# First experts with three mask banks and three buffers of chosen rows, last experts over 71 tiles

## The reference

```python
x = x + _L0_xattn_ref(_layernorm(x), ctx_1024, ctx_1024, ...)     # softmax attention over the context
x = x + _L0_ffn_ref(_layernorm(x), L0_ffn_gate_w, L0_ffn_expert_w)
x = x + _L1_xattn_ref(_layernorm(x), ctx_1024, ctx_1024, ...)     # the same with a causal mask
x = x + _L1_ffn_ref(_layernorm(x), router_w, gate_proj, up_proj, down_proj)

# _L0_ffn_ref: each row goes through the one expert with the highest score (a 128x128 matrix)
scores = jnp.einsum('bsh,eh->bse', x, gate_w)
onehot = jax.nn.one_hot(jnp.argmax(scores, axis=-1), 8)
expert_out = jnp.einsum('bsh,efh->bsef', x, expert_w)
return x + jnp.einsum('bsef,bse->bsf', expert_out, onehot)

# _L1_ffn_ref: each row goes through its best two of 8 experts, F = 352, weighed by their softmax shares
routing_weights, routing_idx = jax.lax.top_k(softmax(x @ router_w), 2)
acts = silu(gate) * up            # 128 -> 352 each
expert_out = acts @ down_proj     # 352 -> 128
```

## Time and profile before

| what | value |
|---|---|
| median of 3 runs (lowest, highest) | 699.16 us (696.54, 702.19) |
| profiled execution, its own time | 697.68 us |
| its span | 695.9 us |
| mean granted TensorE clock | 0.950 |
| busy share of TensorE, VectorE, ScalarE, GpSimd | 86%, 68%, 55%, 49% |

### The profile page before, as it was taken

One profiled execution on the slowest core, in us unless ns is written; L12 is line 12 of the kernel. 1 busy time (PEld: TensorE's weight loads), 2 busy tenths in 40 slices (PEclk: granted clock), 3 DMA queues, 4 the chain that ended last, 5 costly groups with the idle time before them and its releaser, 6 DMA issues.

```text
span 695.9 us, 22954 instructions
## 1 busy us (share of the span) xinstructions
PE 597.2 (86%) x8205; PEld 458.9 (66%) x8205; DVE 476.5 (68%) x1287; ACT 380.1 (55%) x900; POOL 338.0 (49%) x593
## 2 busy tenths in 40 slices
PE   1888399999998999997999988898779999999960
PEld 1555277777664555454667766676569899999960
DVE  2777578888835766677778889888656855555536
ACT  3788167777771344442577676677444344444420
POOL 3666332222412454352333677667638886555540
PEclk9999689999999999998899999999769999999995
DMA  7468827565781055767344423400112232222119
GB/s 192 134 189 193 208 69 158 156 162 147 216 168 59 19 231 159 272 210 279 143 93 113 104 80 93 103 26 29 48 47 77 64 82 71 64 69 67 51 43 351
DMA packets 65407, 87.66 MB, mean 126 GB/s; under 512 B 11528, under 2 KB 52752, under 8 KB 65296
## 3 DMA queue, kind: packets, MB, share of 16 engines
q1 hardware_dynamic: 55736, 74.84, 38.8%
q0 software_dynamic: 4352, 8.99, 4.0%
q10 hardware_dynamic: 5208, 2.36, 1.2%
HBM read 43.99 MB, written 41.96 MB: 124 GB/s over the span
## 4 chain that ended last, share of the span: by engine, by line
PE 56%; DVE 20%; issue 6%; ACT 3%; DMA 2%; SPq 0%; DVEq 0%; ACTq 0%; POOL 0%; POOLq 0%
PE bank L1810 12%; PE bank L814 7%; PE bank L1818 6%; DVE nm L1059 6%; PE bank L1664 5%; PE bank L769 4%; PE bank L795 3%; PE bank L798 3%; PE bank L752 2%; PE bank L835 2%; PE bank L825 2%; PE bank L831 2%; DMA kk<-results 1%; DVE e0ch L1633 1%; PE bank L1459 1%
## 5 line engine op out<-in xcount | busy, mean ns | idle before, releaser
L929 ACT ACTIVATE pr<-bank 128x512 f32<-128x512 f32 x256 | 154.3, 605 | 81.5 <-PE bank L798 78.7
L1059 DVE TENSOR_REDUCE nm<-bank 128x8 f32<-128x1024 f32 x128 | 155.6, 1221 | 33.2 <-PE bank L769 30.3
L1810 PE MATMUL bank<-exxt,qq 128*128 128x128 f32 (+1 forms) x864 | 110.0, 278 | 1.1 <-ACT exxt L1851 0.7
L1810 PEld LDWEIGHTS bank<-exxt,qq 128*128 128x128 f32 (+1 forms) x864 | 101.6, 185 | 2.3 <-ACT exxt L1851 1.1
L1783 POOL DMA_INDIRECT results<-exy,exre x72 | 72.0, 1000 | 25.4 <-issue 25.4
L814 PE MATMUL bank<-pr,wide_values 128*18 128x128 f32 x2048 | 83.0, 281 | 0.0
L1664 PE MATMUL bank<-e0ch,expert_w 128*128 128x512 f32 x128 | 70.5, 633 | 7.4 <-DVE e0ch L1633 7.4
L795 PE MATMUL bank<-qq,kk 48*128 48x128 bf16 x1024 | 75.9, 222 | 0.4 <-ACT pr L929 0.4
L798 PE MATMUL bank<-mt,pick 64*128 64x128 bf16 x1024 | 76.0, 222 | 0.0
L1889 DVE TENSOR_TENSOR exhi<-bank,exsi 128x384 f32<-128x384 f32 x72 | 40.1, 557 | 49.2 <-PE bank L1810 40.3
L1340 POOL DMA_INDIRECT sorted_in<-rrrow,rrpli x64 | 62.9, 983 | 16.5 <-issue 15.3
(11 more groups left out here) (246 smaller groups left out, 1101.1 us busy)
## 6 DMA issues: line engine op xcount, KB each, us to landing
sorted_in<-values SPq DMA_DIRECT2D x25, 715.0 KB, 5.9
kk<-k_parts SPq DMA_DIRECT2D x64, 96.0 KB
qq<-q_parts SPq DMA_DIRECT2D x64, 96.0 KB
exx<-sorted_in SPq DMA_DIRECT2D x72, 65.0 KB
kk<-k_parts SPq DMA_DIRECT2D x64, 64.0 KB
qq<-q_parts SPq DMA_DIRECT2D x64, 64.0 KB
k_parts<-pj_parts SPq DMA_DIRECT2D x8, 384.0 KB, 3.4
q_parts<-pj_parts SPq DMA_DIRECT2D x8, 384.0 KB, 3.7
```

The source lines that it names most:

```text
L929: act.activation(probs[c], st_bank[(n * NC + c) % ST][:], ACT.Exp, scale=scale).then_inc(exp_s, 1)
L1059: dve.tensor_reduce(neg_max[n % 2][:, u * 2 * C4:(u + 1) * 2 * C4], score_banks(n, u).rearrange("q (h k) -> q h k", k=T), AX_X, ALU.max, n ...
L1810: mm = pe.matmul(to[q.p][0:fn, f * T:(f + 1) * T], own_w[q.p][:, w0 + f0:w0 + f0 + fn], x, start=True, stop=True)
```

## The change

Two edits that do not touch each other.

1. **First experts.** The masks get three banks (2, 3 and now 6) and the chosen rows three buffers. TensorE issues spread 2 of a group behind turn_back, ahead of expert 0, and behind expert e it issues spread e+3 where it issued e+2. The waits on banks and buffers reach three back instead of two. Bank 6 held the turned queries of groups 0 to 6; these now go to bank 0, the bank of the turned rows, so turn_queries waits until the turned rows of the group after have been kept, and turn waits until the queries turned before have been kept. The wait for the cross attention's last use of bank 6 moves from turn_queries to spread 2 of the first group.
2. **Last experts.** The loops over tiles end after 71 (64 whole tiles plus at most 7 begun ones). The lists still have 72 slots, the last group still fetches and turns four tiles.

```diff
@@ -40,6 +40,8 @@
 F = 352
 FCH = ((0, 128), (128, 128), (256, 96))
 SLOTS = 2 * B + E
+
+TILES = 2 * B + E - 1
 ROW = D + 2
 LIST = B * T + T
 SPARE = 2 * B * T
@@ -140,6 +142,7 @@
 SURE = 5
 EARLY = (2 * SURE * BMAX - (E - 1)) // G * G
 LATE = SLOTS - EARLY
+SPREAD = 3
 LAST_BATCH, BEFORE_LAST = BATCHES[-1], BATCHES[-2]
 LATE_TURN, LATE_SCORE, LATE_SHARE, LATE_COUNT, LATE_LIST = 3, 5, 8, 9, 11
 
@@ -152,6 +155,7 @@
                 return batch, j // 2, j % 2
     return None
 LAST_TILES = Group(NQ // 2 - 1, 1)
+LAST_TILE = Seq(LAST_TILES, (TILES - 1) % G)
 
 
 class Stage:
@@ -1422,10 +1426,10 @@
             top, best = two("top", [128, G]), two("best", [128, G])
             tie, ranked = two("tie", [128, G, E]), two("rk", [128, G, E])
             hot = two("hot", [128, G, E], BF16)
-            chosen = two("ch", [128, GT])
+            chosen = [sb(f"e0ch{p}", [128, GT], to=own) for p in range(SPREAD)]
             padding = values[0][:].rearrange("p b d -> p (b d)")[:, 0:PAD * ROW].rearrange("p (n d) -> p n d", d=ROW)
             t_bank, sc_bank, hot_bank, y_bank, z_bank, qt_bank, q_bank = (
-                bank[0], bank[1], bank[2:4], bank[4], lambda g: bank[7 if g.n < LAST.n else 4], lambda g: bank[6 if g.n < LAST.n else 4], lambda g: bank[5 if g.n < LAST.n else 4])
+                bank[0], bank[1], (bank[2], bank[3], bank[6]), bank[4], lambda g: bank[7 if g.n < LAST.n else 4], lambda g: bank[0 if g.n < LAST.n else 4], lambda g: bank[5 if g.n < LAST.n else 4])
 
             def x_of(g):
                 return x_res[:, g.n * G:(g.n + 1) * G, :]
@@ -1443,10 +1447,10 @@
                 mm.then_inc(z_ps, 1)
 
             def turn_queries(pe, g):
-                if g.n == 0:
-                    pe.wait_ge(cross.norm_s, B)
                 pe.wait_ge(q_ln.xn_s, g.n + 1)
                 pe.wait_ge(q_kept, earlier(g.n))
+                if g.n < LAST.n:
+                    pe.wait_ge(kept, min(g.n + 3, NG))
                 for t in range(G):
                     mm = pe.transpose(qt_bank(g)[:, t * T:(t + 1) * T], q_ln.xn[g.p][:, t, :], ident[:])
                 mm.then_inc(q_turned, 1)
@@ -1509,6 +1513,7 @@
                     pe.wait_ge(cross.max_s, B * (NC // 2))
                 pe.wait_ge(ln.xn_s, g.n + 1)
                 pe.wait_ge(kept, earlier(g.n))
+                pe.wait_ge(q_kept, earlier(g.n - 2))
                 for t in range(G):
                     mm = pe.transpose(t_bank[:, t * T:(t + 1) * T], ln.xn[g.p][:, t, :], ident[:])
                 mm.then_inc(turned, 1)
@@ -1527,9 +1532,11 @@
                     pe.wait_ge(cross.exp_s, B * NC)
                 if e == 0:
                     pe.wait_ge(hot_s, g.n + 1)
-                pe.wait_ge(chosen_s, earlier(g.n * E + e - 1))
+                if g.n == 0 and e == 2:
+                    pe.wait_ge(cross.norm_s, B)
+                pe.wait_ge(chosen_s, earlier(g.n * E + e - SPREAD + 1))
                 for t in range(G):
-                    mm = pe.matmul(hot_bank[e % 2][:, t * T:(t + 1) * T],
+                    mm = pe.matmul(hot_bank[(g.n * E + e) % SPREAD][:, t * T:(t + 1) * T],
                                    hot[g.p][:, t, e:e + 1].broadcast_to([128, 128]), ident4[:, 0, :],
                                    start=True, stop=True)
                 mm.then_inc(hot_ps, 1)
@@ -1629,8 +1636,9 @@
                 def choose(g, e):
 
                     dve.wait_ge(hot_ps, g.n * E + e + 1)
-                    dve.wait_ge(y_ps, earlier(g.n * E + e - 1))
-                    dve.tensor_tensor(chosen[e % 2][:], hot_bank[e % 2][:], xn_t[g.p][:], ALU.mult).then_inc(chosen_s, 1)
+                    k = (g.n * E + e) % SPREAD
+                    dve.wait_ge(y_ps, earlier(g.n * E + e - SPREAD + 1))
+                    dve.tensor_tensor(chosen[k][:], hot_bank[k][:], xn_t[g.p][:], ALU.mult).then_inc(chosen_s, 1)
 
                 def body(g, first=False, last=False):
                     choose(g, 0)
@@ -1661,16 +1669,17 @@
                     pe.wait_ge(chosen_s, g.n * E + e + 1)
                     if e == 0:
                         pe.wait_ge(y_s, earlier(g.n))
-                    pe.matmul(y_bank[:], expert0_w[:, e, :], chosen[e % 2][:], start=(e == 0), stop=(e == E - 1)
+                    pe.matmul(y_bank[:], expert0_w[:, e, :], chosen[(g.n * E + e) % SPREAD][:], start=(e == 0), stop=(e == E - 1)
                               ).then_inc(y_ps, 1)
 
                 def body(g, first=False, last=False):
                     if not first:
                         turn_back(pe, g.before())
+                    spread(pe, g, SPREAD - 1)
                     for e in range(E):
                         expert(g, e)
-                        if e + 2 < E:
-                            spread(pe, g, e + 2)
+                        if e + SPREAD < E:
+                            spread(pe, g, e + SPREAD)
                         if e == 3 and not last:
                             turn(pe, g.after())
                         if e == 5 and not last:
@@ -1785,7 +1794,7 @@
                         y_g[q.b][:], None).then_inc(y_out[q.b], 16)
 
                 def body(g):
-                    for t in range(G):
+                    for t in range(min(G, TILES - g.n * G)):
                         routed.late_gpsimd(g.n * G + t)
                         send(Seq(g, t))
                 all_groups(pool, body, NQ)
@@ -1842,7 +1851,7 @@
                 body(FIRST, first=True)
                 middle_groups(pe, body, NQ)
                 body(LAST_TILES, last=True)
-                down(Seq(LAST_TILES, G - 1), expert_of(pe, Seq(LAST_TILES, G - 1)))
+                down(LAST_TILE, expert_of(pe, LAST_TILE))
 
             def on_scalar(act):
                 def keep_turned(g):
@@ -1879,7 +1888,7 @@
                 body(FIRST, first=True)
                 middle_groups(act, body, NQ)
                 body(LAST_TILES, last=True)
-                keep_out(Seq(LAST_TILES, G - 1))
+                keep_out(LAST_TILE)
 
             def on_vector(dve):
                 def activate(q):
@@ -1909,9 +1918,9 @@
                     dve.tensor_tensor(result[g.p][:].unsqueeze(2), tags, aside[:].unsqueeze(2), ALU.add).then_inc(tags_s, 1)
 
                 def body(g, last=False):
-                    for t in range(G):
+                    for t in range(min(G, TILES - g.n * G)):
                         activate(Seq(g, t))
-                        if not (last and t >= G - 2):
+                        if g.n * G + t + 2 < TILES:
                             take_weights(Seq(g, t).ahead(2))
                         routed.late_vector(g.n * G + t)
                         if t == G - 1 and not last:
@@ -1929,7 +1938,7 @@
                 body(LAST_TILES, last=True)
 
             stage = Stage(on_sync, on_tensor, on_scalar, on_vector, on_gpsimd)
-            stage.results_out = [(y_out[t], 16 * NQ) for t in range(G)]
+            stage.results_out = [(y_out[t], 16 * len(range(t, TILES, G))) for t in range(G)]
             return stage
 
         def combine(x_dst, ran):
```

## The result

| kernel | median, us | runs (lowest, highest) | profiled execution, its span | clock |
|---|---|---|---|---|
| before | 699.01 | 6 (696.54, 702.19) | 697.68, 695.9 | 0.950 |
| changed | 693.94 | 6 (692.71, 696.12) | 692.71, 690.9 | 0.951 |

The ratio is 0.994, with a 95% interval of 0.9912 to 0.9968. The change makes the kernel faster by 0.3 to 0.9%, less than the 1% that one measurement can tell from no change. The two profiled executions differ by 5.0 us, the medians by 5.1.

The account below looks back on a forecast made before the run. A loop of VectorE and TensorE, closed through ScalarE, was taken to bound the first experts, TensorE the last. Savings of 2.1 us there and 2.0 for the tile gave 699.16 - 4.1 = 695.1 us, range 691.0 to 699.0.

Parts of the forecast that it names:

- The loop that bounds the stage: First experts: VectorE from query_rest to choose 3, TensorE to queries, then ScalarE; one spread less saves 0.22 us a group.
- Zero for the buffers: First experts: the extra bank and buffer gain nothing; choose 5's 0.84 us wait goes, but nobody waits for it.
- The cover before expert 1: First experts: TensorE's 0.59 us wait before expert 1 absorbs the added spread, which delays expert 0 by some 0.05 us.
- The new waits: First experts: turn_queries' wait for keep_turned has 2.1 us of room, turn's wait is for queries long kept; no cost.
- The room at turn: First experts: narrowest place, ScalarE's apply ends at 274.32 and turn starts at 274.45, leaving 0.13 us.
- First group: First experts' opening group: the added spread fits in 0.98 us of idle time before expert 0, so 0.22 us is gained.
- Last group: First experts' final group, without stats: choose 3 and expert 3 come 0.32 us earlier, plus 0.22 us behind expert 3: 0.54 us.
- The tile: Last experts: one tile less saves 2.00 us of TensorE, from below 1.33 us.
- Only the tile counts: First experts: another wait, most likely turn, closes the 0.22 us, leaving 697.2 us; chance 0.12.
- The bubbles are a lack of buffers: First experts: waits before experts 1 and 3 both go, 7.7 us in all, giving 687.4 us; chance 0.07.
- Less low clock: Start of causal attention: the half-clock stretch at 325 to 335 us goes, worth 2.4 us, giving 692.7; chance 0.12.

Follow-up runs that it names:

- The fifth run: Choose 3 put ahead of query_stats in VectorE's list, against the changed kernel: one execution 692.16 us, period 13.74 us.
- e0y: Not a follow-up run: a buffer in the profile rows, read by TensorE's transposes at L1446 and waited for from ScalarE; no measured time of its own.
- the tile alone: The kernel before with 71 tiles in the last experts and nothing else changed: median 696.32 us against 699.77, ratio 0.9967.
- the third run: The changed kernel with three mask banks and three buffers, but each spread at its old place: one execution 695.07 us, period 14.05 us.
- spaced chooses: The changed kernel with GpSimd's bias moved behind row_rstd and VectorE's chooses 1, 2 and 3 each moved earlier: median 688.35 us against 699.39, ratio 0.9846.
- the first experts' part alone: The changed kernel with 72 tiles in the last experts: median 695.6 us against 699.77 of before, ratio 0.9927.
- bias later: The changed kernel with GpSimd's bias of the group before moved behind the next row_rstd: one execution 691.85 us, period 13.77 us.

## Why the prediction was right

The forecast was 695.1 us in a range of 691.0 to 699.0, and 693.94 was measured. In the two traces the stage's 2.37 us are 0.11 up to the first turn_back (0.22 foreseen), 1.69 over the six middle periods (1.32 foreseen) and 0.57 in the last group (0.54 foreseen). Both traces have low clock in the first group and not of the same shape, so the 0.11 can't be split. Point by point:

- **The loop that bounds the stage.** Right. The distance of VectorE's part is unchanged (5.42 us), TensorE's from expert 3 to queries is 0.27 us shorter. One spread accounts for 0.22. The rest is score: behind a spread it was 0.86 us from its start to that of turn_queries, in TensorE's timeline before (277.98 in the earlier trace rows):

```profile
277.12 1.01 PE L1520 MATMUL bank<-gate_w,e0xt 128*128 128x8 f32 x8
```

  Behind an expert it is 0.81 (276.16 to 276.97 above). The others of groups 2 to 6 have 0.86 or 0.87 and 0.81 or 0.82. I had counted the spread and not what the step behind it gains; why score is shorter there is not shown.
- **Zero for the buffers.** Right for the middle groups, shown from both sides: depth without the new place gives a period of 14.05, the new place without the third buffer 13.77. In the last group the third buffer gives 0.23 us. I had put that group's whole 0.54 us on the place of the spread, and a part of it belongs to the buffer, through choose 2.
- **The cover before expert 1.** Right. The wait is still there, and in four of the five groups 2 to 6 it is 0.54 or 0.55 us from the end of the spread's 0.22 us to the expert, where I had expected about 0.5:

```profile
282.57 0.39 PE L1539 MATMUL bank<-ident,e0hot 128*128 128x128 bf16 x4
283.34 1.12 PE L1672 MATMUL bank<-e0ch,expert_w 128*128 128x512 f32 x2 [0.38 <-DVE e0ch L1641]
```

  In the period shown further up it is 0.35. There turn_back is late: one step of route (L1567, at 263.83) took 0.64 us where it takes 0.34 to 0.36 in those others, and choose 7, expert 7 and turn_back came later for it, but query_rest did not. So choose 1 starts 1.48 us behind turn_back (267.38 to 268.86), and started 1.68 us behind it before (267.91 to 269.59). The period did not change, which shows that the cover was enough. A spread behind turn_back starts 0.49 us after it, where I had reckoned with 0.44.
- **The new waits.** Right: neither turn nor turn_queries waits for the other's bank.
- **The room at turn.** 0.13 us was read off rows as if a start could follow an end at once. The fifth run shows that about half of such a distance is the handover. It did not matter at this change, since apply and expert 3 both follow from query_rest: apply starts 5.57 us behind it now (266.40 to 271.97) and started 5.54 behind it before (267.13 to 272.67). It decides the next one.
- **First group.** The added spread fitted into the idle time ahead of expert 0, which is now 0.76 us:

```profile
212.39 1.26 PE L1672 MATMUL bank<-e0ch,expert_w 128*128 128x512 f32 x2 [0.76 <-DVE e0ch L1641]
...
214.16 2.08 PE L1672 MATMUL bank<-e0ch,expert_w 128*128 128x512 f32 x2
```

- **Last group.** Expert 3 comes 4.19 us behind its turn_back and not 4.53. Queries come 0.58 us sooner behind those before them, for 0.54 foreseen:

```profile
308.48 0.65 PE L1446 MATMUL bank<-ident,e0y 128*128 128x128 f32 x4 [0.23 <-ACT e0y L1703]
...
312.67 1.12 PE L1672 MATMUL bank<-e0ch,expert_w 128*128 128x512 f32 x2
```

- **The tile.** 2.00 us foreseen; 2.16 between the first gate_up and the last send, and 2.2 for the tile alone.
- **The rivals.** "Only the tile counts" is refuted by the stage's own 2.37 us and by the period. "The bubbles are a lack of buffers" is refuted by the changed kernel together with the third run, and with it, for this stage, the reading that I had taken from the Trainium skill, "Perfetto Trace Analysis", Optimization Strategy: the gap repeated before expert 3 in every group, and a third bank and buffer left it at 0.42 us. What took it away were two moves in the lists of VectorE and GpSimd. "Less low clock" came in part: the low stretch at the start of the causal attention took 10.2 us of the trace before and 6.8 of the one after, and the stretch up to the first causal output projection was 0.32 us shorter. That it came of the change is not shown. Windows after, which answer to the earlier trace rows:

```profile
325.00:330.00 5.00, 3.02 (x47) 2.22 (x43) 3.56 (x6) 1.13 (x4) 0.00 (x0) 0.59 1.02 416
330.00:335.00 5.00, 5.00 (x93) 3.40 (x87) 2.89 (x3) 1.83 (x5) 1.34 (x2) 0.73 0.88 353
```

Between the 4.1 us foreseen and the 5.0 of the two traces stand 0.3 us of the stage, 0.2 of the tile, 0.3 of the clock and 0.3 behind the last send, less 0.2 lost before the stage; that is 0.9.

## What to carry to other kernels

A wait that comes back in every turn of a loop is read from the engine that feeds it: if that engine has no idle time ahead of its instruction, as here, more banks and buffers don't take the wait away, and the order of its list is the next thing to try. When two ways close a loop within a tenth of a microsecond of each other, neither edit shows anything alone, so try them together before either is dropped; and a distance between a recorded end and a start that depends on it is room only beyond the handover that a waiting pair of the same kind shows. What a spread, a tile or a wait is worth below 1% is read from landmarks between stages of the traces and not from medians, which for the kernel before alone ranged from 697.4 to 699.8 us over the sets of runs.

## What the runs showed of the hardware

- **The same work, and another clock.** Up to the first expert the changed kernel and the one with spaced chooses have the same rows at 212.39 and 212.40 us, both behind 0.76 us of idle time. In the one the clock then fell (the expert took 1.26 us and the next 2.08), in the other it did not, and its row is the one below. Nor did it fall in the first experts' part alone, whose lists up to there are those of the changed kernel.

```profile
212.40 1.12 PE L1674 MATMUL bank<-e0ch,expert_w 128*128 128x512 f32 x2 [0.76 <-DVE e0ch L1643]
```

Leaving out the two kernels with added matmuls there, the low stretch of the first group is absent from five of the seven traces with a spread in that gap (the changed kernel and the one with bias later have it), and present in all three without (before, the tile alone, spreads in the old place). Whether the spread makes the difference stays open; the low stretch is worth about 1.2 us of the stage (108.18 against 106.98 and 107.21 us).

- **Filled gaps and the clock.** With 15 added matmuls at the start of the causal attention the clock was 1.00 through a stretch that had been at 0.50 for 10.2 us in the same kernel without them. Four in one gap of the first group went with a fall 11 us later, where the kernel before has full clock. Each is one trace, and the clock differs between traces of the same lists too.
- **A small matmul's cost differs with what stands ahead of it.** Score, with 8 columns a matmul, took 0.86 us up to the next step where it stood behind a spread's bf16 matmuls, and 0.81 where it stands behind an expert's fp32 ones.
